# Weighted values moved directly behind the scores, and two transposes given other PSUM banks, in a single-core fused transformer kernel

## What is computed

```python
def reference(x, ...):
    x = x + 0.5 * local_block(layernorm(x))      # layers L = 0, 1
    x = x + global_attention(layernorm(x))
    x = x + 0.5 * local_block(layernorm(x))      # layers L = 2, 3
    return x

def _layer(x, ...):                              # 8 heads of 64, windows of 64
    h = shift_token(x)
    q, k, v = split(h @ wqkv)
    q, k = rotary_xpos(l2norm(q) * qs, l2norm(k) * ksc)
    o = local_attention(q, k, v)                 # each window sees itself and the one before it
    x = x + o @ wo
    h = layernorm(shift_token(x)) * lg + lb
    a, g = split(h @ w1 + b1)
    x = x + (a * gelu(g)) @ w2 + b2
    return x
```

## Time and profile before

| | |
|---|---|
| time, median of 3 runs | 3139.74 us (3137.11 to 3140.84) |
| the profiled execution | 3138.16 us, its span 3135.3 us |
| TensorE busy | 3041.9 us, 97% of the span |
| VectorE busy | 2687.8 us, 86% |
| ScalarE busy | 2271.7 us, 72% |
| GpSimd busy | 1675.3 us, 53% |
| chain that ended last | TensorE 92%, VectorE 4%, issue 2%, ScalarE 1% |
| mean granted TensorE clock | 0.991 of full speed |

### The profile page before, as it was taken

The page is one execution under the profiler, slowest core; times in us unless marked ns, Lnnn a source line. Parts: engine busy times, 40 slices in busy tenths (PEclk is TensorE's granted clock), DMA queues, the critical chain, the costliest instruction groups (busy, mean ns, idle before and its releaser), DMA issues.

```text
span 3135.3 us, 84712 instructions
## 1 busy us (share of the span) xinstructions
PE 3041.9 (97%) x31009; PEld 2208.9 (70%) x31009; DVE 2687.8 (86%) x6052; ACT 2271.7 (72%) x5488; POOL 1675.3 (53%) x1000
## 2 busy tenths in 40 slices
PE   5999999999999999989999699999999999999999
PEld 3777777666777777657777477777766677777766
DVE  6999999678999998768999599999966899999866
ACT  4888888537888888328889388888853688888842
POOL 6888886215666665441000588888621466666610
PEclk9999999999999999999999799999999999999999
DMA  4111112201111121200000011111221111111211
GB/s 117 33 35 34 32 37 48 48 20 31 33 36 33 33 45 41 49 8 1 1 1 1 18 35 33 35 33 33 51 48 21 31 33 36 33 33 43 46 38 50
DMA packets 136855, 107.23 MB, mean 34 GB/s; under 512 B 80937, under 2 KB 102402, under 8 KB 136450
## 3 DMA queue, kind: packets, MB, share of 16 engines
q1 hardware_dynamic: 136450, 101.83, 14.4%
HBM read 12.67 MB, written 4.19 MB: 5 GB/s over the span
## 4 chain that ended last, share of the span: by engine, by line
PE 92%; DVE 4%; issue 2%; ACT 1%; SPq 0%; DMA 0%; DVEq 0%; ACTq 0%
PE psum L1168 15%; PE psum L1042 10%; PE psum L1145 7%; PE psum L1190 7%; PE psum L1212 7%; PE psum L1179 7%; PE psum L1097 6%; PE psum L1068 5%; PE psum L1131 4%; PE psum L1226 3%; PE psum L1239 3%; PE psum L1412 3%; PE psum L1388 3%; PE psum L1087 3%; PE psum L1121 2%; PE psum L1398 2%
## 5 line engine op out<-in xcount | busy, mean ns | idle before, releaser
L420 POOL TENSOR_TENSOR rnorm<-ssq_floor,neg_half 128x16 f32<-128x16 f32 x256 | 746.5, 2916 | 687.1 <-DVE qkr L738 653.4
L425 POOL TENSOR_TENSOR qk_cos<-qk_cos,qk_sin 128x1024 f32<-128x1024 f32 x256 | 607.4, 2373 | 0.0
L495 ACT ACTIVATE shared<-psum,neg_max 128x128 f32<-128x128 f32 x2048 | 584.1, 378 | 31.0 <-DVE neg_max L714 30.5
L1168 PE MATMUL psum<-wqkv,hT 128*128 128x512 f32 x1024 | 557.1, 628 | 22.2 <-DVE qk_sin L699 9.8
L699 DVE TENSOR_TENSOR qk_sin<-psum,sin 128x256 f32<-128x256 f32 x1024 | 380.8, 413 | 22.2 <-ACT sq L502 21.4
L502 ACT ACTIVATE sq<-psum 128x512 f32<-128x512 f32 x512 | 318.4, 622 | 110.0 <-PE psum L1168 109.3
L555 ACT ACTIVATE shared<-psum,b1g 128x512 f32<-128x512 f32 (+1 forms) x192 | 131.3, 686 | 351.7 <-PE psum L1042 349.6
L705 DVE TENSOR_TENSOR qk_cos<-psum,cos 128x512 f32<-128x512 f32 x512 | 347.3, 679 | 14.2 <-ACT sq L502 14.0
L530 ACT COPY shared<-psum 128x512 f32<-128x512 f32 x512 | 276.7, 592 | 108.4 <-PE psum L1212 107.9
L1190 PEld LDWEIGHTS psum<-wo,shared 128*128 128x128 f32 x2048 | 267.1, 191 | 123.5 <-issue 123.2
L1042 PE MATMUL psum<-shared,w1g 128*128 128x512 f32 (+1 forms) x768 | 345.8, 593 | 7.2 <-DVE shared L804 5.3
(11 more groups left out here) (131 smaller groups left out, 6508.9 us busy)
## 6 DMA issues: line engine op xcount, KB each, us to landing
vprev<-v SPq DMA_DIRECT2D x512, 130.0 KB, 2.3
shared<-Y SPq DMA_DIRECT2D x32, 256.0 KB
shared<-Y SPq DMA_DIRECT2D x32, 254.0 KB
X<-in_L_attn_x SPq DMA_DIRECT2D x8, 512.0 KB, 6.7
out<-X SPq DMA_DIRECT2D x8, 512.0 KB, 3.5
wqkv<-in_L_ffn_wqkv SPq DMA_DIRECT2D x4, 768.0 KB, 4.8
w<-in_L_ffn_w SPq DMA_DIRECT2D x4, 341.0 KB
wo<-in_L_ffn_wo SPq DMA_DIRECT2D x4, 256.0 KB, 6.4
```

The costliest lines, as they stand in the source:

```text
L420: nc.gpsimd.tensor_tensor(rnorm[:], ssq_floor[:], neg_half[:], ALU.pow).then_inc(rnorm_ready, 1)
L425: nc.gpsimd.tensor_tensor(both, both, qk_sin[:, t.m % 2, :], ALU.add).then_inc(sum_ready, 1)
L495: last = nc.scalar.activation(probs[:, c * P:(c + 1) * P], bank(3 + i, (c % 4) * P, (c % 4 + 1) * P), ACT.Exp, bias=neg_max[:, c:c + 1])
L1168: nc.tensor.matmul(bank(i), hT[:, t.m * P:(t.m + 1) * P], wqkv[:, i * INNER:(i + 1) * INNER], start=True, stop=True).then_inc(qk_psum, 1)
```

## The change

Three steps of TensorE's slot change place, and two change bank.

1. `weigh_values` of tile s-1 stands directly behind `scores`, ahead of `heads_transpose`.
2. `queries_transpose` writes bank 5 (where the projected values and the transposed heads go) instead of bank 2. So `weigh_values` no longer waits for the copy of the queries (`qT_ready`), `heads_transpose` does, and `queries_transpose` waits for the copy of the values.
3. `tokens_transpose` stands at the slot's end, behind `weights_transpose`, for tile s+5 instead of s+4 at the slot's start; for tiles from row 5 on it writes bank 4. So `scores` waits for the copy of these tokens (`hT_ready`), and on ScalarE that copy (`tokens`) stands between the two copies of `weights`.

The slots below 0 keep their order. In slot 0 the tokens of tile 5 are transposed in addition to those of tile 4.

```diff
         def x_bank(t):
-            return 1 if t.L and t.row < 5 else 6
+            return 4 if t.row >= 5 else 1 if t.L else 6
...
         def qT_bank(t):
-            return 1 if t.L and t.row < 2 else 2
+            return 1 if t.L and t.row < 2 else 5
...
             def local_slot(L, s):
-                if t := tile_at(L, s + 4):
+                if s <= 0 and (t := tile_at(L, s + 4)):
                     tokens(t)
...
                 if t := tile_at(L, s):
-                    weights(t)
+                    weights(t, 0)
+                if s >= 0 and (t := tile_at(L, s + 5)):
+                    tokens(t)
+                if t := tile_at(L, s):
+                    weights(t, 1)
...
             def scores(t):
+                if t.row and (u := tile_at(t.L, t.row + 4)):
+                    wait(pe, hT_ready, before(u, 0, 2))
...
             def heads_transpose(t):
                 wait(pe, o_ready, before(t, 0, 2))
-                if u := tile_at(t.L, t.row + 4):
-                    wait(pe, v_ready, before(u, 0))
+                if u := tile_at(t.L, t.row + 3):
+                    wait(pe, qT_ready, before(u, 0))
...
             def weigh_values(t):
-                if u := tile_at(t.L, t.row + 2):
-                    wait(pe, qT_ready, before(u, 0))
...
             def queries_transpose(t):
-                elif t.row < 3:
-                    wait(pe, qT_ready, before(t, 1))
-                elif u := tile_at(t.L, t.row - 3):
-                    wait(pe, o_ready, before(u, 0, 2))
+                elif u := tile_at(t.L, t.row + 1):
+                    wait(pe, v_ready, before(u, 0))
+                else:
+                    wait(pe, oT_ready, before(t, 4))
...
                 elif s < NT:
                     scores(tile(0))
-                    if t := tile(4):
-                        tokens_transpose(t)
+                    weigh_values(tile(-1))
                     if t := tile(-2):
                         heads_transpose(t)
-                    weigh_values(tile(-1))
...
                     weights_transpose(tile(0), 1)
+                    if t := tile(5):
+                        tokens_transpose(t)
                     if t := tile(2):
                         keys_transpose(t)
                         queries_transpose(t)
```

More of the change, by code:

```diff
@@ L523, in values, with weights @@
                 nc.scalar.copy(v[:, t.m % 4, :, 0:DH], heads(bank(v_bank(t)))).then_inc(v_ready, 1)
[L525 to L530, removed]
+            def weights(t, i):
+                cols = slice(i * BANK, (i + 1) * BANK)
+                act.wait_ge(probsT_psum, 2 * t.n + i + 1)
+                wait(act, pv_ready, before(t, 1))
+                nc.scalar.copy(probsT[:, cols], bank(6 + i)).then_inc(probsT_ready, 1)
             def rotated(t):
@@ L1108, in tokens_transpose @@
                     pe.wait_ge(y_ready, (t.L - 1) * NG + t.row // GROUP + 1)
-                if x_bank(t) == 6 and t.row < 5:
+                if x_bank(t) == 6:
                     wait(pe, hT_ready, before(t, 1, 2))
-                elif x_bank(t) == 6:
-                    wait(pe, probsT_ready, 2 * (t.n - 5) + 1)
+                elif x_bank(t) == 4:
+                    wait(pe, probs_ready, 2 * (t.n - 4))
                 elif u := tile_at(t.L, t.row - 3):
@@ L1178, in project_v @@
                     wait(pe, v_ready, before(t, 1))
+                    if u := tile_at(t.L, t.row - 2):
+                        wait(pe, qT_ready, before(u, 0))
                 nc.tensor.matmul(bank(v_bank(t)), hT[:, t.m * P:(t.m + 1) * P], wqkv[:, 2 * INNER:3 * INNER],
@@ L1208, in weights_transpose @@
                     wait(pe, o_ready, before(t, 1, 2))
-                elif u := tile_at(t.L, t.row + 4):
-                    wait(pe, hT_ready, before(u, 0, 2))
                 for c in range(4 * i, 4 * i + 4):
@@ L1267, in local_slot @@
                     weights_transpose(tile(0), 1)
+                    tokens_transpose(tile(5))
                     keys_transpose(tile(2))
```

## The result

| | before | after |
|---|---|---|
| time, median | 3139.28 us (3133.64 to 3141.18, 17 runs) | 3131.52 us (3127.31 to 3134.42, 17 runs) |
| span of the profiled execution | 3135.3 us | 3128.7 us |
| TensorE busy | 3041.9 us, 97% | 3019.2 us, 97% |

The ratio is 0.9978, with a 95% interval of 0.9972 to 0.9984: 7.8 us faster. The forecast was 3131.5 us; that the median meets it to the hundredth is luck, since the changed kernel's own runs lie 7 us apart.

What follows compares the result with a forecast made beforehand. TensorE's own order was taken to set the 8.405 us slot, with a VectorE and GpSimd floor of 8.305 under layer norms. Steady slots -24.4 and layer ends +16.2 give -8.2 us: median 3131.5 us, range 3114 to 3143.

Steps and rivals of the forecast that it cites:

- One change of shape less: TensorE, steady slots: one switch fewer between quarter, half and whole-array products gains 0.19 us a slot without new waits.
- Rival C: TensorE: no drain between quarters and halves, 0.14 us a slot more gained, 3110 us; chance 0.06.
- The heads' copy, 0.08 us back: Values' projection waits for ScalarE's later copy of the heads, taking back 0.08 us; net gain 0.11 us a slot.
- Rival B: Heads' copy is in time for the values' projection: 136 slots gain 0.19 us each, 3121 us; chance 0.14.
- The floor of 8.305 us with a layer norm: Slots with a layer norm: the loop of VectorE and GpSimd allows no period below 8.305 us, whatever TensorE does.
- Steady slots, -24.4 us: 94 layer-norm slots fall from 8.405 to 8.305 us, 9.4 us; 136 others gain 0.11 each, 15.0 us.
- The scores' wait for the tokens: Scores, slot start: the tokens' copies end at 8.08 against a start at 8.30, leaving 0.1 us after the semaphore.
- Rival E: Scores wait for tokens' copies 0.2 us later: period about 8.38 in all 230 slots, 3150 us; chance 0.12.
- Rival F: Small restarts at several waits: steady period falls only 0.05 to 0.07 us, 3142 us, no change; chance 0.14.
- The ends, +16.2 us: Slots 60 to 63: later heads delay copy, exponentials and output projection, 4.05 us a layer, +16.2 us in four.
- Rival D: Layer ends don't pay, for instance because the maxima bound the exponentials: 3115 us; chance 0.04.

Runs made afterwards that it cites:

- statistics first: Changed kernel with the layer norm's two statistics steps ahead of ssq_floor on VectorE from slot 3 on: 3133.35 us, ratio 0.9982 to the kernel before.
- exponentials first: Changed kernel with the first four exponentials ahead of the heads' copy on ScalarE in slots 60 to 63: 3119.04 us, ratio 0.9940 to the kernel before.
- kernel before with the statistics first: Kernel before the change, with the layer norm's statistics steps ahead of ssq_floor on VectorE: 3139.04 us against 3139.17, ratio 0.9999.
- tokens back: Changed kernel with the tokens' transpose of tile s+4 again between scores and weighted values: 3165.49 us, ratio 1.0088 to the kernel before.
- values last: Changed kernel with the values' projection behind both projections of queries and keys on TensorE: 3124.22 us, ratio 0.9958 to the kernel before.
- values last with statistics: Changed kernel with the values projected behind both other projections and the layer norm's statistics ahead of ssq_floor: 3114.89 us, ratio 0.9929 to the kernel before.
- bank back: Changed kernel with the queries' transpose writing bank 2 again, so weighted values wait for the queries' copy: 3255.52 us, one run.
- all three: Changed kernel with exponentials ahead of the heads' copy at layer ends, values projected behind both other projections, statistics ahead of ssq_floor: 3098.32 us, ratio 0.9870.

## Why the prediction was right, step by step

- **One change of shape less, 0.19 us before waits.** Right: the slot without the late wait is 8.21 us against 8.405, and the pieces stand where they were put (0.20 to the weighted values, heads at 2.29, 0.11 for the tokens). The new neighbourhood of quarters and halves costs the same 0.20 as the old ones. Rival C, no drain between them, is out by that row. The drain that the Trainium skill ("TensorEngine Tiling (Array Packing)", "Key Properties") states for each change of mode agrees with it.
- **The heads' copy, 0.08 us back.** Right: L1184 at 1.10 us, its weight load released by that copy, 8.29 against 8.21 us with and without the wait. Rival B is out.
- **The floor of 8.305 us with a layer norm.** Right in size: 8.31 us. The experiment with the statistics first shows the cause. The Trainium skill ("SBUF — State Buffer", "SBUF: two separate sides") tells of a port pair that GpSimd and some of VectorE's operations use in turn, each for a whole instruction; that ssq_floor ends when GpSimd's addition does, and takes 0.16 us when the addition is over, agrees with it. That the ports are the reason was not tested apart.
- **Steady slots, -24.4 us.** Measured -24.2 us, by the table above. Two small misses cancel: the 94 slots with a layer norm gave 8.3 instead of 9.4 us, 0.7 of it because of three single slots of 8.5 to 8.7 us, and the others gave 15.9 instead of 15.0, since their period is 8.29 and slot 59 takes 8.18.
- **The scores' wait for the tokens.** Rival E needed copies 0.15 us later. In the trace after they end at 918.97, and the scores start at 919.19 with the usual gap behind the last transpose: no wait. Rival F, small restarts at several waits, needed a period only 0.05 to 0.07 shorter; it is 0.11 shorter.
- **The ends, +16.2 us.** Right in size: 7.57, 7.57 and 7.13 us against the 7.59, 7.59 and 7.15 forecast, slot 63 1.08 to 1.09 us longer in all four layers, 16.0 us in all without the fall of the clock. Right in mechanism for slots 61 to 63, where the edit of ScalarE's order takes the loss away. Rival D is out. For slot 60 the mechanism was wrong. The prediction lets TensorE wait for the exponentials at the output projection in all of slots 60 to 62, before and after; before the change it waits there only from slot 61 on, and after it slot 60 waits at the values' projection for the copy of the heads instead, which needs the same bank. Both ways put the output projection at 4.77 us, so that the 0.98 us of this slot came out is luck, and putting the exponentials first does not help it.
- **What was not foreseen** is the clock. It fell in slot 61 of layer 2, 1.66 us in the profiled execution. The first three slots of layers 0 and 2 took 0.6 and 0.5 us more, and the clock fits there too: in layer 0 it was at the lower level for the first 1.3 us of slot 0 (51.14 to 52.4) and at the full level there before, in layer 2 until 1783.0 (slot 0 starts at 1779.60), before only until 1785.3 with a slot 0 that starts at 1784.03. The windows view of 49.00 to 52.40, before and then after (columns as in the last section; the granted clock is the third from the end):

```profile
49.00:52.40 3.40, 2.29 (x39) 1.29 (x39) 3.00 (x8) 1.04 (x4) 3.28 (x4) 1.00 0.08 16
49.00:52.40 3.40, 3.27 (x28) 1.58 (x30) 2.51 (x5) 0.08 (x1) 3.21 (x4) 0.50 0.00 0
```

The stretch from slot 63 of layer 1 to layer 2, with the global attention in it, is 531.46 us before and 531.49 after, although slot 63 itself got 1.09 longer; so the rest of it is 1.1 us shorter, at a mean granted clock of 0.97 instead of 0.96. That this is the clock too fits another profile: in the kernel before with the statistics first, which has the same code there, the stretch takes 534.3 us, and the clock is at 0.50 from 1371.8 to 1377.7, where the kernel before has it in full at the same place. With these, the span accounts for itself: -6.5 us in the table, +1.0 in the first slots and -1.1 in this stretch are the -6.6 us between the two profiles.

## What to carry to other kernels

Where TensorE runs without a gap, its time still has slack in the order: put products that use the array in parts side by side, and whole-array work together, since one change cost some 0.15 us here. Then look at who reads what moved: a step that comes later on one engine holds up everything queued behind its reader, and in stretches with less work (here the ends of the layers) that wait has nothing to hide behind. A stretch whose period doesn't follow the engine that was sped up has another loop; an operation that takes six times its usual duration shows where.

## What the runs showed of the hardware

The granted clock fell at the end of a layer, where it had not in the profile before. TensorE in layer 2 after the change, slot 61 (one L1215 group of eight transposes takes 1.04 elsewhere):

```profile
2290.94 1.47 PE L1195 MATMUL psum<-wo,shared 128*128 128x128 f32 x8 [1.81 <-ACT shared L495]
2292.20 1.91 PE L1215 MATMUL psum<-ident,shared 128*128 128x128 f32 x8
```

and the windows view around it (stretch, its length, then busy time and count of TensorE, of its weight loads, VectorE, ScalarE and GpSimd, the granted clock, the share of the DMA engines and GB/s):

```profile
2286.00:2291.00 5.00, 3.19 (x76) 2.50 (x73) 3.22 (x7) 3.14 (x11) 1.99 (x1) 1.00 0.23 52
2291.00:2295.00 4.00, 4.00 (x22) 4.00 (x23) 2.45 (x15) 2.00 (x6) 0.00 (x0) 0.57 0.00 0
```

The mean granted clock was 0.57 from 2291 to 2295, so for most of it the lower of the two levels, 1.2 instead of 2.4 GHz, right behind a wait of 1.81 us. The slot took 9.23 us instead of 7.57. The same wait in layer 0 (1.00 granted from 569 to 573) brought no fall, so it does not always bring one. Counted over the profiles by slots of 60 to 62 that are 1.6 us too long: the six kernels with waits of 1.8 us there (after, tokens back, values last, values last with statistics, statistics first, bank back) have 14 such slots in 24 ends of layers, and the four with waits of at most 1.0 us (before, before with statistics first, exponentials first, all three) none in 16. Slot 63 adds four falls to the six kernels and none to the four. A fall costs 1.66 us (9.23 against 7.57). That the wait is what brings the fall fits these counts, but the wait was not varied by itself. An example, values last with statistics first, in layer 0:

```profile
556.00:560.00 4.00, 3.96 (x21) 3.99 (x22) 2.42 (x14) 2.10 (x6) 0.00 (x0) 0.59 0.00 0
```

So part of what the values' projection gave back was lost there: the kernel with the values projected last had two such slots in its profile and the changed kernel one. Whether these falls also make the spread of the run times is open. The four runs each of the kernels with exponentials first and with all three edits, without such falls, spread by 2 us, and the 17 of the changed kernel by 7; but the kernel before has none in its profile and its 17 runs spread by 7.5 us, and the kernel with the tokens back has three and its four runs spread by 1.7 us.
